# A pre-norm layer with chunked attention and a routed feed-forward on one core: the first seven feed-forward tiles computed inside the attention ticks, their pieces first in each slot

## The chip, the cores and the metric

One NeuronCore of one Trainium2 chip runs the program. Its engines are PE (TensorE), DVE (VectorE), ACT (ScalarE), POOL (GpSimd) and SP (SyncE, which here only issues DMAs). Each engine works through its own list of instructions in order, and the lists are tied together by semaphores. The metric is the device time of one execution, in microseconds, as the median of several.

## The reference

The input x is 2 x 2048 tokens of 256 values, all float32.

```python
x = x + attn(_layernorm(x))
x = x + ffn(_layernorm(x))
...
q, k, v = [silu(causal_dwconv(x @ W, conv)) for each]     # 4 taps, 256 channels, 4 heads of 64
q, k = q / norm(q), k / norm(k); beta = sigmoid(x @ Wb)
A = einsum(K * beta, K) over all heads, in chunks of 64 tokens
T = inverse of (I + tril(A, -1)); W = T @ (K * beta); U = T @ (V * beta)
scan over the chunks: u = U - W * diag(S); S = S + K^T u
    o = Q * diag(S) + tril(q . k) * u
out = (o * rsqrt(mean(o * o) + eps) * g) @ Wo
...
h = gelu(x @ Wfc) @ Wproj for 2 shared experts (all tokens)
  + the same for the 2 best of 8 routed experts (each token), weighted
```

Only the diagonal of S is used later, and `tril` of a matrix of (batch, token in chunk) keeps the token 0 of the first batch and the tokens 0 and 1 of the second. So apart from two "edge" tokens in a chunk, the output of the attention is q times the diagonal of S.

## The kernel before

The work has two stages, one behind the other.

**Attention** (0 to 613 us). The 4096 tokens go in 8 groups of 512, alternating between the two batches. Every group passes four parts, and each part is cut into 19 slots. `run_attention` (L1616) writes the same order for each engine: a *tick* runs slot 0 of all parts, then slot 1, and so on, and the parts of one tick belong to different groups. There are 11 ticks; the first three and the last three lack some parts.

- `ahead` (slots 8 to 18): statistics of the first layer norm on VectorE, the power -1/2 on GpSimd (L732), the scaled x `xn` on ScalarE (L870), its transposes `xnT` (L965), beta.
- `front` (slots 0 to 17): the projections of q, k and v in float32 (L990), their eviction twice on ScalarE, plain and scaled (L812, L813), three convolution steps on VectorE (L1278), silu (L799), the head sums of the squares (L981) and their power on GpSimd (L689), K to token layout (L972), normalized and turned back (KT), then K times beta, A (L1027), the five masked copies `CT` on GpSimd (L697), Q and V.
- `back` (slots 0 to 15): the inverse by doubling, five levels of three products: Y (L1052), Z (L1058) and its transpose ZT (L1059). Then W and U (L1065), their products with K, the sums over chunks and the scan on VectorE (slot 13, L1358 to L1386), the edge tokens, the squares of o. In slot 12 GpSimd splits one piece of the shared weights into a high and a low float16 half (L706 to L710).
- `tail` (slots 0 to 12): o to token layout, normalized, turned back, times Wo (L1106), the residual, the statistics of the second layer norm, its power (L721), `x2n`, its transposes, the router's logits (L1123).

PSUM has eight banks. The parts take theirs in turn from `Ring`s: three for front, three for back, one for tail and ahead together, and the eighth for small sums. A product waits until its bank has been emptied.

**Feed-forward** (613 to 1420 us). A tile is 256 tokens; a *unit* is a tile times one expert. An f32 product is made of three float16 products (high x high, high x low, low x high). A unit has four up groups of 12 products (L1191), each followed by gelu (L902), the high half on ScalarE (L907) and the low half on VectorE (L1555), and then 48 down products (L1206) and one eviction. There are 16 tiles for the two shared experts and 39 routed ones: 71 units. x of each tile is read back and turned on PE (L1175). `shared_order` does the first 8 shared tiles, and meanwhile splits the 32 pieces of routed weights (L929, L1564) and runs the router in nine steps on VectorE (`router`); `routed_order` does the 39 routed tiles, `shared_order` the last 8 shared ones, where the routed rows are gathered and added.

## Time and profile before

| what | us |
|---|---|
| median of 3 runs | 1411.62 (1410.79 to 1422.15) |
| the profiled execution | 1421.95 |
| its span, first to last instruction | 1420.1 |
| attention stage, up to the last logits | 613 |
| a full tick (all four parts) | 65 to 71 |
| feed-forward from its first up group | 797 |

The span is what the trace covers; the execution's time is 1.85 us more. Busy times are those of one execution. TensorE's clock has two levels here, 2.4 GHz (1.00) and 1.2 GHz (0.5); "PEclk" is its mean over a stretch. PE's "busy" counts work at either level. A matmul of float32 operands stands in the trace as two records, a transpose or a float16 matmul as one.

### The profile page before, as it was taken

How to read it: one execution, taken by the hardware profiler on the slowest of the kernel's cores; microseconds unless marked ns; L12 is line 12 of the kernel's file. 1: busy time of each engine (PE TensorE's matmuls, PEld its weight loads, DVE VectorE, ACT ScalarE, POOL GpSimd, SP SyncE). 2: the span in 40 equal slices, each digit the busy share in tenths (PEclk: the TensorE clock that was granted, in tenths of full speed). 3: DMA queues.
4: the chain of work that ended last, by engine and by line, in shares of the span. 5: the costliest groups of instructions: out<-in, count | busy, mean ns of one | idle time of the engine just before them, and what ended most of it. 6: DMA issues, size and time to landing. Idle time of an engine off the chain costs nothing.

```text
span 1420.1 us, 28215 instructions
## 1 busy us (share of the span) xinstructions
PE 1278.8 (90%) x10048; PEld 1117.9 (79%) x10049; DVE 735.0 (52%) x1258; ACT 599.2 (42%) x1081; POOL 360.5 (25%) x335
## 2 busy tenths in 40 slices
PE   4787989889898988569989999999999999999998
PEld 2667787768686867458878889899989999888887
DVE  2556656775767665327785433333333333344554
ACT  3442525252534342055636444444444444453442
POOL 0406162533334244200001022112211221043342
PEclk9787979997988889769999999999999999999999
DMA  2000101010101010043424211111111112133332
GB/s 89 30 1 30 45 30 46 30 60 15 59 15 59 0 60 29 17 129 123 158 74 150 83 38 52 50 46 44 52 51 45 44 51 52 53 106 111 111 109 76
DMA packets 60541, 86.12 MB, mean 61 GB/s; under 512 B 7168, under 2 KB 50432, under 8 KB 60480
## 3 DMA queue, kind: packets, MB, share of 16 engines
q1 hardware_dynamic: 53664, 66.65, 14.5%
q0 software_dynamic: 6816, 18.62, 4.7%
q8 instruction: 42, 0.69, 0.2%
q14 instruction: 19, 0.16, 0.0%
HBM read 60.35 MB, written 24.90 MB: 60 GB/s over the span
## 4 chain that ended last, share of the span: by engine, by line
PE 79%; DVE 8%; issue 6%; ACT 4%; POOL 3%; SPq 1%; DMA 0%; DVEq 0%; POOLq 0%; ACTq 0%
PE ps L1191 26%; PE ps L1206 25%; PE ps L990 4%; PE ps L981 3%; PE ps L965 3%; PE ps L1065 3%; PE ps L1052 2%; PE ps L1059 2%; PE ps L972 2%; PE ps L1058 2%; PE ps L1175 2%; PE ps L1106 2%; DVE W L1278 2%; POOL W L697 1%; PE ps L1143 1%
## 5 line engine op out<-in xcount | busy, mean ns | idle before, releaser
L1191 PE MATMUL ps<-late_room,W 128*128 128x256 f16 x3408 | 387.1, 274 | 7.4 <-DVE late_room L1549 7.4
L1206 PE MATMUL ps<-W,late_room 128*128 (+1 forms) x3408 | 383.2, 273 | 0.0
L1191 PEld LDWEIGHTS ps<-late_room,W 128*128 (+1 forms) x3408 | 334.8, 98 | 48.6 <-issue 4.8
L1206 PEld LDWEIGHTS ps<-W,late_room 128*128 128x128 f16 x3408 | 333.4, 98 | 38.2
L1555 DVE SCALAR_TENSOR_TENSOR late_room<-ps,late_room 128x512 f16<-128x512 f32 x284 | 189.1, 688 | 243.8 <-ACT late_room L907 243.6
L902 ACT ACTIVATE ps<-ps 128x512 f32<-128x512 f32 x284 | 165.4, 583 | 343.7 <-PE ps L1191 343.7
L907 ACT ACTIVATE late_room<-ps 128x512 f16<-128x512 f32 x284 | 161.0, 596 | 0.0
L791 ACT COPY W<-ps 128x512 f32<-128x512 f32 x144 | 82.1, 584 | 141.9 <-PE ps L965 114.2
L1278 DVE SCALAR_TENSOR_TENSOR W<-W 128x512 f32<-128x512 f32 x144 | 114.1, 793 | 24.7 <-ACT W L813 21.3
L743 POOL COPY gath<-idx 128x2 int32 (+1 forms) x39 | 7.1, 182 | 469.2 <-PE ps L1175 324.1
L965 PE MATMUL ps<-idt,W 128*128 128x128 f32 x384 | 72.7, 343 | 44.5 <-ACT W L870 17.4
L965 PEld LDWEIGHTS ps<-idt,W 128*128 128x128 f32 x384 | 59.5, 182 | 51.8 <-issue 24.3
L990 PE MATMUL ps<-W 128*128 128x512 f32 x192 | 99.7, 624 | 0.0
L746 POOL DMA_INDIRECT late_room<-x2n_d,gath x78 | 75.2, 964 | 43.5 <-POOL gath L743 31.6
L1606 DVE TENSOR_SCALAR late_room<-ps 128x512 f32<-128x512 f32 x39 | 27.0, 692 | 108.1 <-PE ps L1206 108.1
L981 PEld LDWEIGHTS ps<-W 128*128 128x128 f32 x384 | 54.2, 228 | 25.5 <-issue 14.9
L697 POOL TENSOR_TENSOR W<-W 128x512 f32<-128x512 f32 x40 | 56.7, 1451 | 66.9 <-ACT W L791 66.9
L981 PE MATMUL ps<-W 128*128 128x2 f32 x384 | 55.3, 278 | 17.8 <-ACT W L802 9.4
L772 POOL DMA_INDIRECT W<-ys_d,lastidx x64 | 61.5, 961 | 36.9 <-POOL lastidx L769 26.0
L812 ACT COPY W<-ps 128x512 f32<-128x512 f32 x48 | 27.9, 582 | 83.3 <-PE ps L990 83.2
L1052 PEld LDWEIGHTS ps<-W 128*128 128x128 f32 x320 | 44.9, 209 | 21.1 <-issue 17.1
L689 POOL TENSOR_TENSOR W<-W 128x16 f32<-128x16 f32 x16 | 46.1, 2897 | 48.6 <-ACT W L823 48.6
(141 smaller groups left out, 1413.0 us busy)
## 6 DMA issues: line engine op xcount, KB each, us to landing
wstage<-in_w_ffn SPq DMA_DIRECT2D x40, 512.0 KB, 3.7
ys_d<-late_room SPq DMA_DIRECT2D x39, 256.0 KB, 2.1
W<-in_x SPq DMA_DIRECT2D x16, 512.0 KB, 3.8
x2n_d<-W SPq DMA_DIRECT2D x8, 512.0 KB, 3.0
base_d<-W SPq DMA_DIRECT2D x8, 512.0 KB, 3.0
late_room<-x2n_d SPq DMA_DIRECT2D x16, 256.0 KB, 4.1
late_room<-base_d SPq DMA_DIRECT2D x16, 256.0 KB, 3.1
acc_d<-late_room SPq DMA_DIRECT2D x8, 256.0 KB, 5.7
```

The costliest lines, as they stand in the source:

```text
L746: pool.indirect_dma_start(out=xg[b][:, c], out_offset=None, in_=x2n_d, in_offset=bass.IndirectOffsetOnAxis(ap=gath[:, b, c:c + 1], axis=0) ...
L791: act.copy(dst, ring.bank(name)).then_inc(ring.empty(n, name)[0], 1)
L902: act.activation(ps[:, c, :], ps[:, c, :], ACT.Gelu, scale=1.0 / (X_SCALE * W_SCALE)).then_inc(gelu_done, 1)
L907: act.activation(hs[b][:, 0, 2 * c:2 * c + 2].rearrange("p f t -> p (f t)"), ps[:, c, :], ACT.Copy, scale=H_SCALE).then_inc(h_high, 1)
L965: by_tile(ring, n, name, lambda to, k: pe.transpose(to, src[:, k, d * P:(d + 1) * P], idt[:]))
L981: last = pe.matmul(dst[:, at:at + P // HD], src[:, d, k * P:(k + 1) * P], headsel, start=True, stop=True)
L990: mm = pe.matmul(to, wqkv[:, d, m * P:(m + 1) * P], xnT[:, d], start=(d == 0), stop=(d == DB - 1))
L1052: by_tile(bk, n, f"Y{s}", lambda to, k: pe.matmul(to, CT[:, s - 1, k], X[:, k], start=True, stop=True))
L1191: last = pe.matmul(ps[:, c, f * XT:(f + 1) * XT], weight(slot, d, hw, cols), xs[t.par][:, hx, d], start=(q == 0), stop=(q == len(parts) - 1))
L1206: last = pe.matmul(ps[:, 4 + b, c * D:(c + 1) * D], hs[b][:, hh, f, c * P:(c + 1) * P], weight(slot, DB + f // 4, hw, cols), start=(q == 0 ...
L1278: dve.scalar_tensor_tensor(qkvT[:, m], pre[:, m, t:t + GRP], cw[:, m, t:t + 1], qkvT[:, m], ALU.mult, ALU.add).then_inc(conv_step, 1)
L1555: dve.scalar_tensor_tensor(lo, ps[:, c, :], H_SCALE, hi, ALU.mult, ALU.subtract).then_inc(h_low, 1)
```

## The change

The attention and the order of the feed-forward are rewritten.

- **Feed-forward inside the attention.** The first half (256 tokens) of each of the groups 0 to 6 is a "fed" tile. Its x comes from `x2nT` of the tail directly, so it isn't read back and turned. One tick after its tail its eight up groups go into slots 8 to 15 (`up_piece`, two PSUM banks in turn), and one tick later its four down groups into slots 1, 3, 5 and 6 (`down_piece`). In each slot the pieces come ahead of the attention's parts, on every engine. That is 14 of the 71 units.
- **12 ticks of 16 slots**, all written out, none in a loop: tick t has ahead of group t, front of t-1, back of t-2, tail of t-3, up of t-4 and down of t-5. The scan is now in slot 2 of the tail.
- **Less attention work.** The projections take three float16 products instead of a float32 one, and give beta too, spread over its head, as a tanh (`gate`). Q, V and K times beta are no longer turned to token layout: q's norm is needed on the edge tokens alone (`edges`, its power on GpSimd behind the masks), since the rest is divided out by the last norm. The inverse keeps X and makes its transpose on PE (`XT`, evicted by ScalarE) instead of a third product. W and U become one product ZK. The last norm is spread over columns by `rms`.
- **Rings:** two banks each for front, back and tail, two for the pieces; ahead shares one of the tail's.
- **Shared weights** are split on ScalarE and VectorE in ticks 1 and 2 instead of on GpSimd.
- **Behind the attention** (`late_units`): 5 early shared tiles (10 units) with the router in eight steps, 39 routed tiles, 4 final shared tiles (8 units): 57 units and 48 turns. The last 14 pieces of routed weights are loaded and split in the first five routed units (`LOADS`), and every expert gets at least one tile. In the final tiles 8 rows a tile are combined.

The diff, cut to its core (the part classes of Tile, the SyncE lists and the layout of memory are left out):

```diff
+PROJ = 4 * DB
+PROJ_ORDER = (2, 3, 6, 7, 4, 5, 0, 1)
+CONV_ORDER = (2, 3, 4, 5, 0, 1)
...
+FED = 7
+FED_ROWS = [row_tile(n, 0) for n in range(FED)]
+REST_ROWS = [row_tile(n, 1) for n in range(FED)] + [row_tile(n, h) for n in range(FED, GROUPS) for h in range(GRP // XT)]
+EARLY = 5
+FINAL = len(REST_ROWS) - EARLY
...
+LOADS = [2] * 9 + [0] * (N_SH * EARLY - 9) + [3, 3, 3, 3, 2]
...
 FRONT_FILLS = (
-    [(f"proj{m}", "act") for m in range(3 * DB)]
+    [(f"proj{m}", "act") for m in PROJ_ORDER[:5]]
+    + [("ssq", "act")]
+    + [(f"proj{m}", "act") for m in PROJ_ORDER[5:]]
     + [(f"tokK{h}", "dve") for h in range(2)]
-    + [(f"{c}T{d}", "act") for c in ("K", "Kb") for d in range(DB)]
-    + [("AT", "act")]
-    + [(f"tokQ{h}", "dve") for h in range(2)]
-    + [(f"QT{d}", "act") for d in range(DB)]
-    + [(f"tokV{h}", "dve") for h in range(2)]
-    + [("X", "dve")]
+    + [(f"KT{d}", "act") for d in range(DB)]
+    + [("AT", "dve"), ("edges", "act"), ("X", "act")]
 )
 BACK_FILLS = (
-    [(f"{w}{s}", "act" if w == "Y" else "dve")
-     for s in range(1, LEVELS) for w in ("Y", "Z", "ZT") if (w, s) != ("Z", LEVELS - 1)]
-    + [(f"{w}T{d}", "dve") for w in ("W", "U") for d in range(DB)]
+    [("Y1", "act"), ("Z1", "dve")]
+    + [(f"{w}{s - (w == 'XT')}", "dve" if w == "Z" else "act") for s in range(2, LEVELS) for w in ("Y", "XT", "Z")]
 )
 TAIL_FILLS = (
-    [(f"otok{h}", "dve") for h in range(2)]
-    + [(f"oT{d}", "act") for d in range(DB)]
+    [(f"ZK{d}", "dve") for d in range(DB)]
+    + [("corr", "dve"), ("oss", "dve")]
+    + [(f"rms{d}", "dve") for d in range(DB)]
     + [(f"attn{h}", "dve") for h in range(2)]
     + [(f"x2nT{d}", "act") for d in range(DB)]
+    + [("logits", "dve")]
 )
-AHEAD_FILLS = [(f"xnT{d}", "act") for d in range(DB)] + [("beta", "act")]
-SLOTS_A = 19
-W_SLOT = 11
+AHEAD_FILLS = [(f"xnT{d}", "dve") for d in range(DB)]
+SLOTS_A = 16
+DOWN_SLOTS = {1: (0, 0), 3: (0, 1), 5: (1, 0), 6: (1, 1)}
+UP_SLOT = SLOTS_A - 4 * N_SH
...
+def run_attention(front, back, tail, ahead, down=None, up=None, extra=None):
+    for t in range(GROUPS + 4):
+        for slot in range(SLOTS_A):
+            for stage, n, last in ((down, t - 5, FED), (up, t - 4, FED), (back, t - 2, GROUPS), (tail, t - 3, GROUPS),
+                                   (front, t - 1, GROUPS), (ahead, t, GROUPS)):
+                if stage and 0 <= n < last:
+                    stage(slot, n, n % BATCH)
...
+            def front(slot, n, b):
+                if slot == 4:
+                    pool.wait_ge(*fr.empty(n, "ssq"))
+                    pool.tensor_tensor(ssq, ssq, minus_half[:, 0:GT * NH], ALU.pow).then_inc(rnorm, 1)
+                if slot == 9:
+                    pool.wait_ge(at_kept, n + 1)
+                    if n:
+                        pool.wait_ge(*bk.full(n - 1, f"Y{LEVELS - 1}"))
                     for s in range(1, LEVELS):
                         pool.tensor_tensor(CT[:, s - 1], AT, masks[:, s].unsqueeze(1).to_broadcast([P, GT, P]),
                                            ALU.mult).then_inc(masked, 1)
...
-                n = 2 * it + b
+                if slot == 11:
+                    pool.wait_ge(*fr.empty(n, "edges"))
+                    kept_edges = esq[:, 0:DB * GCH * (b + 1)]
+                    pool.tensor_tensor(kept_edges, kept_edges, minus_half[:, 0:DB * GCH * (b + 1)], ALU.pow).then_inc(enorm, 1)
...
-            def ahead(slot, b, it):
-                n = 2 * it + b
-                if slot == 9:
+            def ahead(slot, n, b):
+                if slot == 11:
                     pool.wait_ge(stats, 3 * n + 3)
                     pool.tensor_tensor(rstd, rstd, minus_half[:, 0:GT], ALU.pow).then_inc(rstd_ready, 1)
...
+            def back(slot, n, b):
                 if slot < 10:
                     s = slot // 2 + 1
                     if slot % 2 == 0:
-                        pe.wait_ge(masked, (LEVELS - 1) * n + s)
-                        pe.wait_ge(*(fr.empty(n, "X") if s == 1 else bk.empty(n, f"Z{s - 1}")))
-                        by_tile(bk, n, f"Y{s}", lambda to, k: pe.matmul(to, CT[:, s - 1, k], X[:, k], start=True, stop=True))
+                        if s == 1:
+                            pe.wait_ge(masked, (LEVELS - 1) * (n + 1))
+                            pe.wait_ge(*fr.empty(n, "X"))
+                        else:
+                            pe.wait_ge(*bk.empty(n, f"Z{s - 1}"))
+                        by_tile(bk, n, f"Y{s}", lambda to, k: pe.matmul(to, CT[:, s - 1, k], X[b][:, k], start=True, stop=True))
+                        if s > 1:
+                            by_tile(bk, n, f"XT{s - 1}", lambda to, k: pe.transpose(to, X[b][:, k], idt[:]))
                     else:
+                        pe.wait_ge(*bk.empty(n, f"Y{s}"))
                         if s > 1:
-                            pe.wait_ge(*bk.empty(n, f"ZT{s - 1}"))
-                        pe.wait_ge(*bk.empty(n, f"Y{s}"))
-                        if s < LEVELS - 1:
-                            by_tile(bk, n, f"Z{s}", lambda to, k: pe.matmul(to, XTr[:, k], Y[:, k], start=True, stop=True))
-                        by_tile(bk, n, f"ZT{s}", lambda to, k: pe.matmul(to, Y[:, k], XTr[:, k], start=True, stop=True))
-                if slot == W_SLOT:
+                            pe.wait_ge(*bk.empty(n, f"XT{s - 1}"))
+                        by_tile(bk, n, f"Z{s}", lambda to, k: pe.matmul(to, XTr[:, k], Y[:, k], start=True, stop=True))
...
+            def up_piece(slot, n, b):
+                if slot >= UP_SLOT:
+                    e, c = divmod(slot - UP_SLOT, 4)
+                    u = N_SH * n + e
+                    if slot == UP_SLOT:
+                        if not n:
+                            pe.wait_ge(w_split, SH_PIECES)
+                        pe.wait_ge(fed_low, n + 1)
+                    if e == 0 and c < 2 and n:
+                        pe.wait_ge(y_out, N_SH * (n - 1) + c + 1)
+                    elif 4 * u + c >= 2:
+                        pe.wait_ge(h_low, 4 * u + c - 1)
+                    up_part(u, c, e, xs[n % 2])
+            def down_piece(slot, n, b):
+                if slot in DOWN_SLOTS:
+                    e, c = DOWN_SLOTS[slot]
+                    if c == 0:
+                        pe.wait_ge(h_low, 4 * N_SH * n + 4 + 3 + e)
+                    last = down_part(e, c, e)
+                    if c == XB - 1:
+                        last.then_inc(down_done, 1)
...
+            def ahead(slot, n, b):
+                if slot == 10:
+                    dve.wait_ge(xl_in[b], 16 * (n // BATCH + 1))
                     layer_stats(n, xl, bn, mv, rstd, stats)
-                if slot == 10:
+                if slot == 11:
                     dve.wait_ge(rstd_ready, n + 1)
                     dve.scalar_tensor_tensor(nmr, mv[:, :, 0], -1.0, rstd, ALU.mult, ALU.mult).then_inc(nmr_ready, 1)
```

The removed `run_attention`:

```diff
-def run_attention(eng, front, back, tail, ahead):
...
-        for slot in range(SLOTS_A):
-            for stage, at in ((back, b), (tail, t), (front, f), (ahead, a)):
```

VectorE's new order in the slots that the prediction walks through: slot 0 tail (ZB, product with K); slots 1, 2, 4, 5, 6, 7 one convolution each of K, K, V, V, Q, Q, behind the back's addition and, in slot 2, behind the whole scan; slot 8 low half, additions of the attention output, K times beta, edges; slot 9 low half, last addition, second statistics, X's transpose; slot 10 low half, nmr2, first statistics; slot 11 low half, nmr; slot 12 low half, the edges of q; slot 13 low half, halves of xnT. ScalarE has silu in slots 2, 3, 5, 6, 7 and 8 (silu(1), for Q), tanh in slots 1 and 2, and gelu in slots 8 to 15.

## Rows read from the trace of the kernel before

**Rows 1.** The page: PE's busy time, and its clock in 40 slices
```profile
PE 1278.8 (90%) x10048; PEld 1117.9 (79%) x10049; DVE 735.0 (52%) x1258; ACT 599.2 (42%) x1081; POOL 360.5 (25%) x335
...
PEclk9787979997988889769999999999999999999999
```
**Rows 2.** Windows (stretch, length, busy PE, PEld, DVE, ACT, POOL, PEclk, DMA share, GB/s)
```profile
68.70:139.90 71.20, 58.94 (x326) 49.18 (x325) 42.03 (x73) 24.41 (x45) 23.99 (x12) 0.81 0.05 16
...
276.20:345.20 69.00, 60.64 (x360) 51.50 (x359) 45.52 (x87) 27.95 (x52) 25.73 (x14) 0.84 0.12 39
...
546.00:586.00 40.00, 27.96 (x202) 25.85 (x200) 19.29 (x44) 7.80 (x14) 11.75 (x6) 0.87 0.12 40
586.00:613.00 27.00, 14.65 (x52) 11.03 (x52) 5.07 (x15) 5.70 (x9) 3.12 (x3) 0.63 0.11 39
...
623.00:1420.00 797.00, 779.78 (x7100) 699.53 (x7100) 373.14 (x566) 368.62 (x659) 151.04 (x213) 0.99 0.25 77
```
**Rows 3.** Timeline of PE in a full tick (start, length, engine, line)
```profile
287.01 1.05 PE L1058 MATMUL ps<-W 128*128 128x128 f32 x8
287.90 1.06 PE L1059 MATMUL ps<-W 128*128 128x128 f32 x8
...
290.52 1.02 PE L990 MATMUL ps<-W 128*128 128x512 f32 x2
291.38 1.05 PE L1052 MATMUL ps<-W 128*128 128x128 f32 x8
...
298.82 0.60 PE L965 MATMUL ps<-idt,W 128*128 128x128 f32 x4
299.25 1.02 PE L990 MATMUL ps<-W 128*128 128x512 f32 x2
```
**Rows 4.** Timeline of PE at the start of the feed-forward
```profile
623.12 7.14 PE L1191 MATMUL ps<-late_room,W 128*128 128x256 f16 x48 [1.51 <-DVE late_room L1549]
630.10 0.60 PE L1175 MATMUL ps<-idt,late_room 128*128 128x128 f32 x4
630.53 5.40 PE L1191 MATMUL ps<-late_room,W 128*128 128x256 f16 x48
635.77 5.40 PE L1206 MATMUL ps<-W,late_room 128*128 128x256 f16 x48
```
**Rows 5.** Groups by line, feed-forward, ScalarE and VectorE
```profile
L1555 DVE SCALAR_TENSOR_TENSOR late_room<-ps,late_room 128x512 f16<-128x512 f32 x284 | 189.1, 688 | 243.8 <-ACT late_room L907 243.6
L902 ACT ACTIVATE ps<-ps 128x512 f32<-128x512 f32 x284 | 165.4, 583 | 343.7 <-PE ps L1191 343.7
L907 ACT ACTIVATE late_room<-ps 128x512 f16<-128x512 f32 x284 | 161.0, 596 | 0.0
```
**Rows 6.** VectorE in the attention: a group by line, then its timeline
```profile
L1278 DVE SCALAR_TENSOR_TENSOR W<-W 128x512 f32<-128x512 f32 x144 | 114.1, 793 | 24.7 <-ACT W L813 21.3
...
301.11 1.40 DVE L1250 BATCH_NORM_STATS2 W<-W 128x6 f32<-128x256 f32 x4
...
324.16 2.28 DVE L1360 TENSOR_REDUCE W<-W 128x32 f32<-128x2048 f32 x1
...
328.91 0.19 DVE L1386 TENSOR_TENSOR W<-W 128x32 f32<-128x32 f32 x1
```
**Rows 7.** ScalarE in the attention, by line
```profile
L813 ACT ACTIVATE W<-ps,W 128x512 f32<-128x512 f32 x48 | 33.3, 694 | 0.0
```
**Rows 8.** Timeline of GpSimd in a full tick
```profile
303.32 1.02 POOL L732 TENSOR_TENSOR W<-W 128x4 f32<-128x4 f32 x1 [4.25 <-DVE W L1257]
...
330.93 7.10 POOL L697 TENSOR_TENSOR W<-W 128x512 f32<-128x512 f32 x5 [9.51 <-ACT W L791]
337.99 2.92 POOL L714 TENSOR_TENSOR W<-W 128x16 f32<-128x16 f32 x1
```
**Rows 9.** Timeline of ScalarE at the first silu
```profile
31.77 1.28 ACT L799 ACT_TABLE_LOAD   x1
33.07 0.63 ACT L799 ACTIVATE W<-W 128x512 f32<-128x512 f32 x1
```

More of the change, by code:

```diff
@@ L1438, in _ @@
-            run_attention(dve, front, back, tail, ahead)
-            dve.wait_ge(logits_kept, GROUPS)
-            dve.drain().then_inc(kept, 1)
+                if slot == 13:
+                    for d in range(DB):
+                        dve.wait_ge(xnT_high, DB * n + d + 1)
+                        dve.scalar_tensor_tensor(xnT[:, 1, d], ah.bank(f"xnT{d}"), X_SCALE, xnT[:, 0, d],
+                                                 ALU.mult, ALU.subtract).then_inc(ah.empty(n, f"xnT{d}")[0], 1)
@@ L1441, in _ @@
+            run_attention(front, back, tail, ahead, down=down_piece, up=up_piece, extra=split_piece)
+            dve.wait_ge(*tl.empty(GROUPS - 1, "logits"))
+            dve.sem_inc(kept, 1)
             dve.wait_ge(route_in, 16 * ROUTE_IN)
```

1593 lines of the change are left out of this document (846 added, 747 removed).

## The prediction

> **What bounds the kernel now.** I read the busy shares first: PE is busy 90% of the span, so its work and its clock come before all else [rows 1]. The windows by stage say where that holds. From 623 us on (the feed-forward stage, 71 units) PE works 780 of 797 us at clock 0.99; nothing but fewer units makes that shorter. In the attention stage (0 to 613) a full tick (tail, back, front, ahead) takes 69.0 us, with PE busy 60.6 of them at a mean clock of 0.84 [rows 2]. "Busy" misleads there, since part of it is work at half clock. The PE timeline gives the price at full clock: 8 records of an f32 128-column product take 0.89 us (287.01 to 287.90), 2 records of a 512-column one 0.86, 4 transposes 0.43 [rows 3]. A tick counted with these prices from the code is 49 us, so about 20 of its 69 us are waits and half clock. That is the room into which the change puts feed-forward work. In this stage VectorE is busy 45.5 of 69 us, ScalarE 28, GpSimd 26 [rows 2]: none is full, and the tick is set by chains across all four.
>
> **The late stage.** One unit is 48 up and 48 down products, 5.24 us each (630.53 to 635.77), so 10.48; a turn of x is 0.43 [rows 4]. Before: 71 units 744, 55 turns 24, together 768; 29 us of the 797 are something else: the first group at half clock (7.14 instead of 5.40, and the half clock goes on until the second turn), waits for the router's VectorE work, the end. After: 57 units 597, 48 turns 21. Of the other 29 I take off 7 (PE comes warm from the last down pieces) and add 5, because the router now has 10 early units for 8 longer steps instead of 9 in 16 units. That makes 645. The routed weights no longer are all split beforehand; three pieces a unit in the first routed units fit beside a unit (by LOADS each expert's four pieces are split a unit or more before they are first needed), so I cost it at nothing. The gathers of the last stage (12 before the first combine) hold VectorE some 9 us, while PE has two groups of 5.24 it may run; 0 to 5 us, I take 0.
>
> **PE work in a tick.** Removed per group: transposes of Q, V, Kb, o (48), the 5 ZT products, half of W/U, the Q head sums, beta. Added: 16 XT and 8 rms transposes, one Z, edges. In records: 24 fewer transposes (2.6 us), 48 fewer f32 product records (5.3), some 28 fewer small ones at about 0.11 (3.1): 49 becomes 38 us [rows 3]. The projection goes from 24 records of 0.43 to 48 f16 products; by the feed-forward's 109 ns for 256 columns they are 0.22 each, 10.5 for 10.3: no change [rows 4]. The fed units add 2 x 10.48 = 21. So a full tick holds 59 us of PE at full clock. It can't be shorter than that.
>
> **The chain of a tick.** I walked through the new slots with durations of before, each engine in its order. ScalarE evictions 0.58, scaled 0.69 [rows 7], silu 0.63 [rows 9], gelu 0.58, high half 0.60, VectorE low half 0.69 [rows 5], a convolution of three steps 2.33 (3 x 0.79) [rows 6], additions from PSUM as the low half, hand-overs 0.1, behind a PE group 0.25 (a rounding: 8 records are shown as 1.05 us, the next group starts after 0.89 [rows 3]). From PE's start of slot 0:
> - Slots 0 to 3: VectorE has ZB and the K product until 5.6, waits for Z1 behind the first down piece (9.5), convolves (11.9), then has the whole scan of tail slot 2 (it was 324.2 to 329.1 [rows 6]; two more small steps, 5.8) and only then the second K convolution: 20.1. The K squares are there at 21.4. PE has done its three slots at 17.5 and waits 4 us.
> - Slots 4 to 7: PE is the limit, with 2 x 2.62 of down pieces, four products of the inverse, sums and three projections; each projection needs its bank back from ScalarE (two banks now, three before). tokK is turned at 40.2, K is turned back at 42.9. Here the down pieces are hidden by nothing but also displace nothing: without them the same slots would wait for ScalarE and the pow of 2.9.
> - Slots 8 and 9: up pieces go first on every engine. VectorE comes late (conv 1 at 47.8), does low 0, both attention adds, KbT (1024 columns; bounds 0.8 as one convolution step and 1.6 as two, I take 1.4, since it has twice the columns), the edges: 51.8. AT is on PE until 53.2, kept at 54.0. low 1, Z5, 3X-2I and the second layer statistics end at 57.2 (statistics are 1.40 plus 0.7 [rows 6]).
> - GpSimd decides the rest. Its order is rstd2, the five masks, the edge norms, rstd. From rows: 1.02, 7.10 and, for 16 columns, 2.92 [rows 8]. The edge norm of an odd group has 32 columns, which nothing in the trace shows; bounds 2.92 (as 16) and 5.84 (twice 16); 4 columns cost 1.02 and 16 cost 2.92, so by that slope 5.4, which I take. So rstd is there at 57.2 + 1.0 + 7.1 + 2.9 (5.4) + 1.1 = 69.4 (71.9).
> - VectorE stands at nmr in slot 11 for that, and low 4 is queued behind it; behind low 4, PE's up piece of slot 14. Then nmr, xn (four halves of an eviction, 2.1), its turn (2 x 0.43 and 0.25, 1.1), gelu 5 and high 5, x2nT, the halves of xnT, logits and the last up piece: PE starts the next tick at 77.3 (even) or 79.8 (odd).
>
> So a full tick grows from 69 to 78 or 80 us, with 21 us of feed-forward in it; PE is idle or at half clock for 20 again, now mostly in slots 10 to 14. The eight up pieces are hidden by the GpSimd chain; would that go, they are worth their 10.5.
>
> **Table loads.** The trace shows the load before the first silu: 31.77, 1.28 us, and silu starts at 33.07 [rows 9]. Whether gelu and silu share a table no row says. If not, slot 8 has gelu, then silu(1), slot 9 gelu again, and silu comes back in slot 2: four loads in each of the five ticks with both. I put all four in the walk; two lie in waits, two delay low 1 by about 1 us. Bounds: 0 and 5.1 us a tick; I take 1. The Trainium skill (ScalarE: Activation LUTs, What ACT_TABLE_LOAD costs and Table sets) lists gelu as the anchor of a set of its own and has a switch cost 1283 ns plus a drain of about 1380, and its rule is to batch by set, which speaks against pieces ahead of silu(1). By that price the five ticks would be up to 28 us longer in sum, near 1348 instead of 1320. This trace shows the 1.28 and, with 0.02 us between load and silu, no drain; the measurement decides.
>
> **The sum.** Until the first projection 24 (as before, beta is gone, the projection weights are split instead). Tick 1 (front alone): 48, walked in the same way; four weight splits stand in it on ScalarE and VectorE. Tick 2: 55 (it was 71.2 [rows 2], with a weight split and two pows on GpSimd and the Q and V transposes behind AT). Tick 3 (tail, no feed-forward): 67. Tick 4 (up only) 76, ticks 5 to 7: 78, 80, 78, tick 8 (no ahead, so no wait for rstd, but q_edges waits for the 5.4) 74. Tick 9 (tail, back and both kinds of pieces) 48, where it was 40.0 without them [rows 2]; tick 10 41, where the tail alone, without scan and W, was 27.0 [rows 2]; tick 11 has down pieces only, 10.5, and hides the loading of the router's constants. Hand-over 4. Together 683; with 645: a span of 1328 against 1420, or 1330 against the 1421.95 of the profiled execution, 6.5% less. The median of the runs shown is 0.7% below that execution (1411.62), so I predict 1320. What a measurement of this kernel can tell from no change is about 1%.
>
> **Rivals.**
> - A, PE becomes the bound (17%). The chain in my walk is shorter than it seems, ticks 4 to 7 shrink to 59 to 62, the others by 4 to 10. For it: PE has 59 us of work, and dense f16 work keeps clock 0.99 in the late stage [rows 2]. Against: the masks' 7.1 and the pows [rows 8] stand in one queue before rstd. Attention 577, total 1222, by the median 1214.
> - B, the waits add up more (11%): half clock in the sparse slots stretches PE's share of slots 4 to 7, six ticks get 12 us longer, 683 + 72 + 645 = 1400, by the median 1391. For it: PEclk below 9 in much of the attention stage [rows 1].
> - C, slower (6%): each piece costs its whole round trip. Up piece 1.31 + 0.25 + 0.58 + 0.60 + 0.69 = 3.4, with hand-overs 3.5; eight of them 28, down 10.5, y 1.4: 40 us a tick on top of the old one, with nothing of the attention's own chain got shorter but PE's 11. Seven ticks x 40 minus 8 x 11 = 192: 613 + 192 + 645 = 1450, median 1441. The point from which the change loses is 613 + 7y + 645 = 1420: y = 23 us a tick, hardly more than the 21 of pure PE time. Against it: PE's 20 us of waits and half clock in a tick, and two banks for up pieces.
>
> My forecast (a span of 1270 to 1370, that is 1262 to 1362) has 62%; 4% lies elsewhere. The range 1245 to 1385 leaves out most of A and C and part of B. Faster by over 1%: forecast, A, and most of B, 0.90; within 1% 0.04; slower 0.06.
>
> **What would show it.** Late stage: starts near 683, 645 long, units of 10.48. Ticks of 76 to 80 with PE busy near 65 of them; if they are 62, A; if PE idles at each up piece for VectorE's low half, C. The longest wait in a tick must be VectorE's at nmr for GpSimd's pow, after the masks; if rstd is waited for less than 2 us, my chain is wrong there. PE waits some 4 us for K's head sums. About 20 loads of tables more. GpSimd busy about 30 us a tick. Wrong would also be a first idle of over 10 us at the start of the late stage, or waits of PE for the routed weights.

## The result and the profile after

The change makes the kernel slower: 1439.51 us (median of 4 runs, 1437.88 to 1440.70) against 1413.66 for the kernel before beside it, a ratio of 1.0199 with a 95% interval of 1.0157 to 1.024. I had predicted 1320, in a range of 1245 to 1385, with 6% for slower. In this section the columns of the windows are those of [rows 2], and those of a timeline those of [rows 3].

The page of the kernel after: the engines' busy times and PE's clock in 40 slices.
```profile
PE 1182.4 (82%) x9412; PEld 1014.4 (71%) x9413; DVE 714.4 (50%) x1194; ACT 650.3 (45%) x1150; POOL 356.4 (25%) x284
...
PEclk9797968789788897889889999899999999999999
```
PE has 96 us less to do than before [rows 1], and the span is 1436.8 instead of 1420.1. So 113 us more than before go by without PE. The windows say where: one full tick (381.8 to 476.4), the attention ticks, the late stage.
```profile
381.80:476.40 94.60, 71.49 (x486) 59.10 (x485) 48.90 (x88) 44.68 (x79) 27.57 (x13) 0.82 0.09 28
53.00:759.00 706.00, 524.34 (x3591) 438.30 (x3592) 371.10 (x665) 323.08 (x572) 208.85 (x102) 0.83 0.11 34
759.00:1437.00 678.00, 637.33 (x5735) 565.87 (x5732) 322.35 (x493) 305.91 (x543) 142.81 (x170) 0.98 0.29 87
```
A full tick takes 94.6 us where it took 69.0 [rows 2]. The first instruction of ScalarE in each tick's front (L908) marks the ticks: they start at 25.5, 78.8, 131.5, 204.6, 290.5, 381.8, 476.4 and 565.7, and the late stage's first turn is at 759.4.

| us | predicted | measured | off by |
|---|---|---|---|
| start | 24 | 25.5 | +1.5 |
| ticks 1, 2, 3 | 48, 55, 67 | 53.3, 52.7, 73.1 | +9.1 |
| ticks 4 to 7 | 76, 78, 80, 78 | 85.9, 91.2, 94.7, 89.3 | +49.1 |
| ticks 8 to 11, hand-over | 177.5 | 193.7 | +16.2 |
| attention | 683 | 759.4 | +76 |
| late stage | 645 | 677.4 | +32 |

That tick in lines. PE starts its slot 0 at 379.31. The second K convolution of VectorE runs beside an addition of GpSimd, and the statistics that GpSimd waits for end at 442.3:
```profile
379.31 1.92 PE L1199 MATMUL ps<-W 128*128 128x128 f32 x8
397.67 4.29 DVE L1433 SCALAR_TENSOR_TENSOR W<-W 128x512 f32<-128x512 f32 x3
399.07 2.34 POOL L799 TENSOR_TENSOR W<-W 128x1024 f32<-128x1024 f32 x1 [11.61 <-ACT W L979]
442.10 0.17 DVE L1410 TENSOR_SCALAR W<-W 128x4 f32<-128x4 f32 x1
```
GpSimd at the end of the tick:
```profile
442.35 1.01 POOL L807 TENSOR_TENSOR W<-W 128x4 f32<-128x4 f32 x1 [21.32 <-DVE W L1410]
443.32 6.30 POOL L779 TENSOR_TENSOR W<-W 128x512 f32<-128x512 f32 x5
449.58 5.42 POOL L785 TENSOR_TENSOR W<-W 128x32 f32<-128x32 f32 x1
454.96 1.01 POOL L817 TENSOR_TENSOR W<-W 128x4 f32<-128x4 f32 x1
455.94 2.00 POOL L811 TENSOR_TENSOR W<-W 128x1024 f32<-128x1024 f32 x1
```
VectorE's nmr, ScalarE's xn and the eviction of x2nT by ScalarE:
```profile
456.00 1.95 DVE L1603 SCALAR_TENSOR_TENSOR W<-W 128x4 f32<-128x4 f32 x1 [8.22 <-POOL W L817]
457.99 2.07 ACT L1013 ACTIVATE W<-late_room,W 128x256 f32<-128x256 f32 x4 [9.52 <-DVE W L1603]
461.07 1.07 ACT L876 COPY W<-ps 128x512 f32<-128x512 f32 x2
```
and PE after it:
```profile
462.24 1.08 PE L1111 MATMUL ps<-idt,W 128*128 128x128 f32 x4 [12.91 <-issue]
464.74 1.11 PE L1111 MATMUL ps<-idt,W 128*128 128x128 f32 x4 [1.41 <-DVE W L1608]
465.65 2.77 PE L1277 MATMUL ps<-late_room,W 128*128 128x256 f16 x12
468.21 3.42 PE L1257 MATMUL ps<-W 128*128 128x8 f32 x16
471.48 2.72 PE L1277 MATMUL ps<-late_room,W 128*128 128x256 f16 x12
473.99 1.92 PE L1199 MATMUL ps<-W 128*128 128x128 f32 x8
```
The queue rstd2, masks, edge norm, rstd is the one of my walk, and the 5.42 for 32 columns is my 5.4. But PE is idle for 12.91 us before it turns xn. xn is complete at 460.1, and PE starts only at 462.24: by the code the turn waits until the bank that it shares with x2nT has been emptied, and that eviction, which ends at 462.14, stands on ScalarE behind xn and behind the gelu and the high half of an up piece. Then PE turns the two halves of xn one after the other, as there is one bank for them. The up pieces that follow, 12 products each, take 2.56 and 2.51 from start to start, where a quarter of a group of 48 is 1.31 [rows 4]: the granted clock from 462 to 474 is 0.50.

The late stage: PE's waits of over 4 us for the low half of x.
```profile
853.40 6.72 PE L1277 MATMUL ps<-late_room,W 128*128 128x256 f16 x48 [5.70 <-DVE late_room L1757]
...
896.54 7.31 PE L1277 MATMUL ps<-late_room,W 128*128 128x256 f16 x48 [4.95 <-DVE late_room L1757]
914.17 7.04 PE L1277 MATMUL ps<-late_room,W 128*128 128x256 f16 x48 [4.64 <-DVE late_room L1757]
931.55 6.89 PE L1277 MATMUL ps<-late_room,W 128*128 128x256 f16 x48 [4.66 <-DVE late_room L1757]
948.93 6.74 PE L1277 MATMUL ps<-late_room,W 128*128 128x256 f16 x48 [4.82 <-DVE late_room L1757]
```
The four from 896.54 on are the routed units with three weight pieces each, which I had costed at nothing: some 4.8 us of wait and 1.6 of half clock, four times, 25 us. ScalarE shows why, in the first of them:
```profile
893.49 1.06 ACT L1077 ACTIVATE W<-wstage 128x1024 f16<-128x1024 f32 x1 [4.07 <-DMA wstage<-in_w_ffn]
894.45 0.58 ACT L1057 ACTIVATE late_room<-ps 128x512 f16<-128x512 f32 x1
```
It waits 4.07 us for the third piece to land and splits it (L1077), and only then comes the high half of the next x (L1057), for which VectorE's low half and PE wait in turn.

### The profile page after: what moved, and what is told of

It is laid out like the page before. It is cut to its first block, busy times and chain, and to the rows that moved or that the text cites. A ratio compares the mean times of both kernels' runs of the same rounds, so it can differ in the third digit from the quotient of the medians.

```text
span 1436.8 us, 25329 instructions
## 1 busy us (share of the span) xinstructions
PE 1182.4 (82%) x9412; PEld 1014.4 (71%) x9413; DVE 714.4 (50%) x1194; ACT 650.3 (45%) x1150; POOL 356.4 (25%) x284
## 4 chain that ended last, share of the span: by engine, by line
PE 59%; issue 12%; DVE 11%; POOL 9%; ACT 5%; DMA 3%; SPq 0%; POOLq 0%; DVEq 0%; ACTq 0%
PE ps L1277 22%; PE ps L1286 20%; POOL W L779 4%; PE ps L1137 3%; PE ps L1127 2%; POOL W L785 2%; PE ps L1199 2%; DVE W L1433 2%; PE ps L1111 2%; POOL W L803 1%; PE ps L1257 1%; DMA wstage<-in_w_ffn 1%; PE ps L1206 1%; DVE W L1524 1%; PE ps L1343 1%
## 5 line engine op out<-in xcount | busy, mean ns | idle before, releaser
L1277 PE MATMUL ps<-late_room,W 128*128 128x256 f16 x3408 | 414.1, 283 | 39.3 <-DVE late_room L1757 28.9
L1022 ACT ACTIVATE ps<-ps 128x512 f32<-128x512 f32 x284 | 165.4, 583 | 395.1 <-PE ps L1277 394.8
L1111 PE MATMUL ps<-idt,W 128*128 128x128 f32 x256 | 43.7, 323 | 124.0 <-issue 55.7
L1137 PE MATMUL ps<-W 128*128 128x512 f16 x384 | 100.2, 406 | 1.5 <-DVE W L1608 1.5
L876 ACT COPY W<-ps 128x512 f32<-128x512 f32 x112 | 61.3, 588 | 60.6 <-PE ps L1199 37.3
L1199 PE MATMUL ps<-W 128*128 128x128 f32 x320 | 54.9, 327 | 35.5 <-DVE W L1482 35.5
L860 POOL DMA_INDIRECT W<-ys_d,pos_i x64 | 62.7, 979 | 69.5 <-DMA ys_d<-late_room 50.3
L1199 PEld LDWEIGHTS ps<-W 128*128 128x128 f32 x320 | 50.5, 237 | 41.3 <-DVE W L1482 39.5
L1137 PEld LDWEIGHTS ps<-W 128*128 128x128 f16 x384 | 39.9, 108 | 41.2 <-issue 11.5
L1482 DVE TENSOR_TENSOR W<-W,ps 128x512 f32<-128x512 f32 x40 | 27.3, 682 | 74.4 <-PE ps L1206 74.4
L893 ACT ACTIVATE W<-ps 128x512 f32<-128x512 f32 x48 | 28.7, 598 | 68.7 <-PE ps L1137 67.8
```

Source lines behind the costliest of these rows:

```text
L860: pool.indirect_dma_start(out=yrow[k % YROWS][:, c], out_offset=None, in_=ys_d, in_offset=bass.IndirectOffsetOnAxis(ap=pos_i[:, c, t:t + 1 ...
L1022: act.activation(up_bank(n, c), up_bank(n, c), ACT.Gelu, scale=1.0 / (X_SCALE * W_SCALE)).then_inc(gelu_done, 1)
L1111: by_tile(ring, n, name, lambda to, k: pe.transpose(to, src[:, k, d * P:(d + 1) * P], idt[:]))
L1137: last = pe.matmul(to, wp[:, hw, d, m * P:(m + 1) * P], xnT[:, hx, d], start=(q == 0), stop=(q == len(parts) - 1))
L1199: by_tile(bk, n, f"Y{s}", lambda to, k: pe.matmul(to, CT[:, s - 1, k], X[b][:, k], start=True, stop=True))
L1277: last = pe.matmul(up_bank(n, c)[:, f * XT:(f + 1) * XT], weight(slot, d, hw, cols), x_halves[:, hx, d], start=(q == 0), stop=(q == len(pa ...
```

## The experiments

"Attention" is the start of the late stage's first turn, "late" the rest of the span; both are read from the one profiled execution, while the median is over all. The runs were made in six sessions, each on one chip. In four of them PE gets its instructions slowly in the final shared tiles, in two it doesn't (the last part of this section). That is worth 35 to 40 us (less in e3), and the column "slow feed" tells it, so totals are to be compared within one kind. Runs of one session: the changed kernel; e1 to e4; e5 to e8; e9 to e12; e13 to e16; e17 and e18.

| run | median us | ratio to before (95%) | attention | late | slow feed |
|---|---|---|---|---|---|
| changed kernel | 1439.51 | 1.0199 (1.0157 to 1.024) | 759.4 | 677 | no |
| e9, the same | 1441.65 | 1.021 (1.0141 to 1.0279) | 764.6 | 676 | no |
| e17, the same | 1478.74, one run | | 764.4 | 712 | yes |
| e1 rstd early | 1427.09 | 1.0129 (1.0064 to 1.0193) | 712.3 | 712 | yes |
| e2 attention first | 1449.34, one run | | 734.4 | 713 | yes |
| e3 no pieces | 1514.10, one run | | 692.3 | 820 | yes, for 20 us |
| e4 two loads | 1451.40 | 1.0288 (1.0219 to 1.0357) | 764.3 | 685 | yes |
| e5 ahead early | 1405.92 | 0.9931 (0.9892 to 0.997) | 685.4 | 716 | yes |
| e6 all early | 1377.88 | 0.9738 (0.9672 to 0.9804) | 685.8 | 690 | yes |
| e7 paced gathers | 1427.03 | 1.0114 (1.0081 to 1.0146) | 713.6 | 710 | yes |
| e8 PE shifted | 1435.86 | 1.017 (1.0098 to 1.0241) | 714.3 | 716 | yes |
| e10 plain rows | 1383.86, one run | | 712.0 | 670 | no |
| e11 all early, attention first | 1304.43 | 0.9224 (0.916 to 0.9288) | 655.8 | 651 | no |
| e12 all early, silu | 1333.00, one run | | 679.2 | 652 | no |
| e13 as e6 | 1376.91 | 0.9727 (0.9669 to 0.9784) | 687.8 | 689 | yes |
| e14 as e1 | 1432.24, one run | | 713.9 | 716 | yes |
| e15 as e11 | 1344.53 | 0.951 (0.9464 to 0.9556) | 654.2 | 689 | yes |
| e16 as e2 | 1446.62 | 1.0253 (1.0204 to 1.0302) | 728.1 | 714 | yes |
| e18 as e10 | 1384.62, one run | | 712.8 | 670 | no (e17 beside it: yes) |

**The end of the tick.** In e1 the statistics, the pow and nmr of the group ahead get earlier slots:
```
 POOL ahead (pow of rstd)      if slot == 11  ->  6
 DVE  ahead (statistics)       if slot == 10  ->  5
 DVE  ahead (nmr)              if slot == 11  ->  8
```


> The changed kernel with the first layer norm's statistics in VectorE's slot 5 (before: 10), their power on GpSimd in slot 6 (before: 11, behind the masks and the edge norms) and nmr in slot 8. Theory Q (GpSimd's queue sets the tick): in the tick at 380.6 nmr waited until 456.0, and xn, xnT, low 4, up 6, the logits and up 7 came behind it. Without that only q_edges in slot 12 still waits for the edge norms (455.0), so the next tick starts 3 to 5 us behind 455 and not at 474: the ticks of the changed kernel get 10 to 16 us shorter, those with pieces as well as those without, in all 60 to 90 us: 1350 to 1380. Theory P (the pieces' own round trips set the tick): nmr's wait goes, the pieces stay as slow as they are, and less than 20 us are gained: 1420 to 1440.

Attention fell by 52 us (764.3 in e4, which has the same attention as the changed kernel and ran beside it, to 712.3; against the first profile's 759.4 it is 47). That is a little less than the 60 to 90 expected, and far more than the rival's 20. The total, 1427, would have pointed at the rival: 35 us of slow feed had come in. The whole step early, xn and its turn too, is e5; the edits to PE's waits protect the bank that xnT shares with the tail:
```
 ACT xn  slot 12 -> 9;  PE, ACT, DVE xnT  slot 13 -> 11
 PE, before xnT:    wait for x2nT{DB-1} of tail n-3  ->  wait for attn1 of tail n-3
 PE, before x2nT1:  + wait for ah.empty(min(n + 3, GROUPS - 1), "xnT1")
```


> As the run with rstd early, but the whole layer-norm step ahead comes early: normalising in slot 9, its two transposes on PE, the high and the low half in slot 11 (before 12 and 13), so the two transposes through the one bank stand in front of the second layer norm's and not behind it. Theory 'the end of a tick is a chain that nothing covers' (xn, two transposes through one bank, then PE at half clock): each of the five full ticks is 5 to 8 us shorter than the 82 to 87 of the run with rstd early; attention 712 becomes 670 to 685. Rival 'the chain of the second layer norm ends as late': ticks stay within 2 us, attention 705 to 712. If the final shared tiles are again fed slowly, the late stage stays at 712; without that it would be 677: total 1385 to 1400 by the first theory, 1420 to 1427 by the rival.

Attention 685.4: another 27 us, at the edge of the first theory's 670 to 685, in the same conditions of the late stage (716 against 712). Together the two moves give back 74 to 79 us of attention, about as much as the walk had missed. The full ticks take 80.3, 81.7 and 78.3 (ticks 5 to 7), which is the length that the walk had given to ticks with the queue still in them.

**Two loads a unit, and the edge queries.** e4 splits at most two routed weight pieces a unit: `LOADS = [2] * 9 + [1] + [2] * 6 + [1]`.

> The changed kernel with the last pieces of routed weights two a unit over units 10 to 16 (LOADS [2]*9+[1]+[2]*6+[1]) instead of three a unit. Theory L: in the changed kernel PE waits 4.6 to 5.0 us for x's low half in four routed units (896, 914, 932, 949) and then runs their first group at half clock (6.7 to 7.3 instead of 5.4), because the third piece waits for a buffer and its DMA and ScalarE's x high half is queued behind it. With two a unit the waits go: 22 to 27 us less, 1412 to 1418, the attention stage unchanged. Rival: the waits come from the gathers (two a tile) and stay: within 5 us of 1439.5.

Its late stage is 685 against 712 and 713 of e1 and e2 beside it, 27 us less. VectorE's low half of x makes PE wait 9.6 us in all instead of 28.9. Its 1451 is above the changed kernel's 1439 because some 35 us of slow feed came on top. e6 has it too, with everything early, and VectorE's slot 12 (edge queries) moved to 15.

> As the run before it, plus the two remedies that aim at other terms: two weight pieces a unit as in the run with two loads (that took 19 of the 29 us of waits of PE for x's low half away), and VectorE's product of the edge queries, which waits for GpSimd's edge norms, in slot 15 in place of 12, so that the low halves of the last up pieces do not stand behind it (it waited 5.8 us in an odd tick). If both terms are real, the late stage has 20 to 26 us less and the odd ticks 4 to 6 us less: 1360 to 1375, below the kernel before (1408). If the slow feeding of the final shared tiles costs what the waits for weights gave back, 1380 to 1400.

Late is 25 us shorter than in e5; attention stays at 685.8, so moving the edge queries gained nothing.

**The order, which is what the change is about.** e2 turns the stages of a slot round and nothing else:
```
-  (down, t - 5, FED), (up, t - 4, FED), (back, ...), (tail, ...), (front, ...), (ahead, ...)
+  (back, ...), (tail, ...), (front, ...), (ahead, ...), (down, t - 5, FED), (up, t - 4, FED)
```


> The changed kernel with the attention's parts ahead of the pieces in each slot, on all engines. Theory Q: the pieces' place costs little, since rstd is late anyway. In slots 8 and 9 two table loads fall away (2.6 us of ScalarE a tick), the second statistics no longer wait for low 1, and low 4 stands behind nmr either way: 2 to 4 us a tick in five ticks, 10 to 20 in all: 1420 to 1430. Theory P: with the pieces behind, the chain is freed of their round trips and a tick falls by 10 or more: 1390 or less. That the pieces stand better ahead would be above 1445.

> The changed kernel with the attention's stages ahead of the pieces in every slot, and nothing else, once more: it had attention 734 and a late stage of 713 with the stretches. Without them 734 + 678 = 1412 to 1416, a tie with the kernel before (1411); with them 1449.

Attention is 734.4 (e2) against 764.3 (e4 beside it), and 728.1 in e16. Both totals stand above the changed kernel's 1439, and e2's 1449 lies above the 1445 that was to mean that the pieces stand better ahead; the slow feed again. Where the time goes is clearer tick by tick. The first three ticks have no pieces and take up to 10 us more or less in executions of the same attention, so the last column counts from tick 5 on:

| attention, us | tick 4 | 5 | 6 | 7 | 8 to the end | 5 to the end |
|---|---|---|---|---|---|---|
| changed kernel | 85.9 | 91.2 | 94.7 | 89.3 | 193.7 | 468.9 |
| e2 | 90.2 | 82.1 | 84.7 | 82.3 | 184.1 | 433.2 |
| e16 | 86.5 | 82.0 | 84.7 | 82.3 | 184.1 | 433.1 |
| e6 | 74.1 | 80.3 | 81.6 | 78.3 | 189.0 | 429.2 |
| e11 | 74.9 | 71.4 | 71.4 | 71.5 | 181.9 | 396.1 |

The pieces ahead cost 33 to 36 us. Tick 4, which has up pieces and no down pieces, gains nothing from the other order; every tick with down pieces from 5 to 7 gains 7 to 10. So it is the place of the down pieces that costs. The other order also saves 10 of the 20 table loads, but two of them fall in tick 4, where no time was gained, so they aren't the reason. e11 and e15 ask the question again with everything early.

> As the run with everything early (1378), with the order of the stages within a slot turned round: back, tail, front, ahead, then the down and up pieces. It asks the question of the change once more, with the end of the tick out of the way. If the order is worth what it was in the first pair (attention 25 us shorter than the changed kernel), 1350 to 1360. If that gain and the one of the early step are the same gain, because both come from the chain to rstd, 1375 to 1385.

> Everything early with the attention's stages first, once more. Without the stretches 1304 again (attention 656, late 651). With them, by 'session', 1304 + 38 = 1342; by 'program' 1304. The difference in attention to everything early with feed-forward first should be the 30 us of before (656 against 686) in any session.

655.8 against 685.8 (e6, in another session), and 654.2 against 687.8 (e13) on one chip: again 30 to 34, so this gain adds to the other. e11 and e15 are one program; it beats the kernel before by 7.8% without the slow feed and by 4.9% with it. One full tick of e6 and then of e11:
```profile
336.90:418.50 81.60, 69.13 (x486) 57.91 (x486) 46.53 (x89) 44.43 (x79) 27.57 (x13) 0.88 0.08 24
```
```profile
331.00:402.40 71.40, 64.47 (x486) 54.20 (x485) 44.88 (x90) 41.38 (x78) 27.61 (x13) 0.93 0.12 38
```
The same 486 products, 4.7 us less "busy" since fewer of them run at half clock, and 5.5 us less idle. VectorE's waits for the inverse's products Z (L1485, released by PE L1206) shrink. In e6 they were, with their number and the longest,
```profile
DVE W L1485 <- PE ps L1206: 13.3, 2, 9.2
```
and in e11
```profile
DVE W L1485 <- PE ps L1206: 2.7, 2, 1.5
```
In the whole attention stage VectorE waits 74.4 us for Z in the changed kernel and 25.8 in e16. The lines show how one piece of 2.6 us grows to a wait of 9. In e6, the second K convolution, PE's next product of the inverse (Y), and PE's window after it:
```profile
353.01 4.29 DVE L1436 SCALAR_TENSOR_TENSOR W<-W 128x512 f32<-128x512 f32 x3
358.55 2.07 PE L1199 MATMUL ps<-W 128*128 128x128 f32 x8 [4.74 <-DVE W L1485]
357.00:370.00 13.00, 11.45 (x58) 9.32 (x59) 3.75 (x6) 4.84 (x9) 2.90 (x1) 0.61 0.00 0
```
and the same in e11:
```profile
343.82 2.32 DVE L1436 SCALAR_TENSOR_TENSOR W<-W 128x512 f32<-128x512 f32 x3
347.08 1.06 PE L1199 MATMUL ps<-W 128*128 128x128 f32 x8
345.00:352.00 7.00, 7.00 (x61) 6.17 (x59) 4.68 (x7) 5.42 (x12) 3.83 (x2) 1.00 0.00 1
```
With the pieces ahead, the first Z product comes 2.6 us later (VectorE waits 4.16 for it instead of 1.53). VectorE's second K convolution now falls beside GpSimd's addition and takes 4.29 instead of 2.32. PE has by then done the pieces of slots 1 and 3 and waits 4.74 us for VectorE's addition of Z, and the work behind that idle time runs at a clock of 0.61. With the attention first, a down piece fills this wait and the clock stays at 1.00. The long convolution is in every full tick of e6 and of the changed kernel, and in none of the ticks 5 to 7 of e11 and e16; what it costs by itself, apart from the piece and the half clock, wasn't tested.

**No pieces at all.** e3 takes the fed units out (FED = 0), so that the new attention runs alone.

> The new attention with no pieces in its ticks (FED 0): all 16 shared tiles behind it, 8 early and 8 final, and two pieces of weights a unit. Theory Q: GpSimd's queue stands without pieces too, ticks 3 to 7 take 70 to 76 us as tick 3 of the changed kernel (73.1), the attention ends at 620 to 650 and the rest takes 795 to 805: 1420 to 1450. So the new attention is no faster than the old one (613) though PE has 11 us less in a tick, and the pieces cost 12 to 20 us a tick for 21 us of PE work. Theory P: ticks of 58 to 66, attention end below 590, total below 1395.

Its full ticks take 76 to 81 us and its attention 692, where 620 to 650 was expected. One tick:
```profile
290.70:371.70 81.00, 55.62 (x294) 45.92 (x294) 42.24 (x76) 29.96 (x59) 25.02 (x13) 0.71 0.08 27
```
Here PE's clock is 0.71. That was the surprise of the study: the restructured attention, with nothing in its gaps, is slower than the old one (69.0 [rows 2]), though it has fewer products. 21 us of pieces (10.5 in tick 4) then add only 8 to 15 to a tick. What I had called "room" was there; what was wrong was the tick without them. The early step of e5 wasn't run without pieces.

**Table loads.** e12 is e6 with silu in the fed units in place of gelu, so its feed-forward computes another function.

> As the run with everything early, but the fed units' gelu is a silu (so their activation is another function), which should share its table with the attention's silu if the four table loads of a tick come from gelu. Then the four loads of 1.28 us are gone in five ticks; my walk put 1 us of each tick's 5.1 on the path: attention 3 to 8 us shorter than 661. If the loads are all hidden, 0; if all are on the path, 25 us.

Of the 20 loads at L885 and L1022 one is left, 24 us less for ScalarE, and attention is 6.6 us shorter (679.2 against 685.8, one execution each). So gelu and silu do not share a table, and the walk's sum of 5 us was about right. Its place was not: ticks 4 to 7 are 1 us shorter together, and the rest is gained from tick 8 on.

**Instructions that come one by one.** In e1, e2 and e4 PE was idle again and again in the last 120 us, and in e3 from 1333 to 1354, "issue" being all that the trace names. The same stretch in e17, which is the changed kernel once more:
```profile
1354.17 5.74 PE L1286 MATMUL ps<-W,late_room 128*128 128x256 f16 x47
1360.35 0.28 PE L1286 MATMUL ps<-W,late_room 128*128 128x256 f16 x1 [0.44 <-issue]
1360.47 0.38 PE L1277 MATMUL ps<-late_room,W 128*128 128x256 f16 x2
1361.77 0.60 PE L1277 MATMUL ps<-late_room,W 128*128 128x256 f16 x4 [0.92 <-issue]
1363.19 0.37 PE L1277 MATMUL ps<-late_room,W 128*128 128x256 f16 x1 [0.83 <-issue]
```
while GpSimd issues its indirect gathers without a pause:
```profile
1351.88 0.94 POOL L860 DMA_INDIRECT W<-ys_d,pos_i  x1 [49.89 <-DMA ys_d<-late_room]
1353.13 0.94 POOL L860 DMA_INDIRECT W<-ys_d,pos_i  x1 [0.30 <-issue]
```
Three ways to take it away. e7 has 4 row buffers for 8 (`ACCS, YROWS = 6, 4`), so that fewer gathers are issued ahead; e8 has `for _ in range(64): pe.wait_ge(kept, 1)` ahead of the late stage, both on top of e1.

> As the run with rstd early, but 4 row buffers in place of 8, so that GpSimd issues at most 8 gathers (10 us) ahead of VectorE's combining in place of 16 (20 us). Theory 'PE's instructions come slowly while GpSimd issues gathers without a pause': the four stretches of trickling matmuls get half as long, 45 us become 15 to 25, 1400 to 1410. Rival 'the stretches belong to the layout of this program and not to the gathers': 1427 as before. If the combining itself gets later because fewer rows are there, PE should not notice, as its banks come free from VectorE within a unit.

> As the run with rstd early, but PE executes 63 more waits on a semaphore that is already there, ahead of its late stage, which moves every later PE instruction by 63 places and costs some 3 us at most. Theory 'gathers': the stretches of trickling matmuls in the final shared tiles stay, 1424 to 1432. Rival 'place of the PE instructions in their pages': they go or move, and with them up to 45 us: 1385 to 1420.

Neither helped: late 710 and 716 against 712 in e1 (the session before). Then e10 takes plain copies of consecutive rows for the gathers, and so leaves out the gathering by position; it stands on top of e1 too:
```
-  pool.indirect_dma_start(out=yrow[k % YROWS][:, c], ..., in_offset=bass.IndirectOffsetOnAxis(ap=pos_i[:, c, t:t + 1], axis=0))
+  pool.dma_start(yrow[k % YROWS][:, c], ys_d[(2 * k + c) * P:(2 * k + c + 1) * P, :])
```


> As the run with rstd early, but in the final tiles GpSimd's 64 indirect gathers of rows are 64 plain copies of 128 consecutive rows each, of the same size from the same tensor (so the final rows are combined with wrong partners: the gathering by position is left out). Theory 'the indirect gathers starve PE of instructions': no matmul waits on 'issue', the late stage is 668 to 680, 1380 to 1392. Rival 'the DMA traffic as such': the stretches stay, 1420 to 1430. Rival 'layout of the program': either.

It was gone (late 670), but it was gone in e9, e11 and e12 on that chip too, in programs that keep the gathers, so this proved nothing.

> The changed kernel itself, unaltered, on the chip on which the experiments ran. Its first profile shows no stretch of trickling matmuls in the final shared tiles, where all eight experiments do. If that belongs to this program, it is 1435 to 1442 again, with a late stage of 677. If the stretches depend on how a kernel is placed or started and not on the program, it may come out 30 to 35 us longer, 1465 to 1475, with a late stage near 712; then the experiments' gains over it are that much larger than they seemed.

> The run with everything early once more, unaltered. The eight runs of the first two sessions all had stretches of trickling matmuls in the final shared tiles, the four of the third session had none, the changed kernel among them. Theory 'a property of the chip or the session, not of the kernel': in a session without the stretches this kernel takes 686 + 652 = 1338 to 1342, as the silu variant's late stage has it; in one with them 1376 again, and then the next runs have them too. Rival 'a property of the program': 1376 here whatever the neighbours do.

> The run with rstd early once more, in the session of the three others, to set the plain copies' 1382 against it. 'Session': 712 + 677 = 1389 without the stretches, 1424 with them. 'Program': 1424 in any case, and the plain copies were what took them away.

In the next session, on another chip, all four kernels had it, e15 among them, 40 us above e11 with the same program. The last pair, on yet another chip, tells more:

> The changed kernel a third time. It serves to tell which kind of session this is: without the stretches of trickling matmuls 1437 to 1445 and a late stage of 676, with them 1470 to 1485 and a late stage near 712.

> The plain copies in place of the indirect gathers (so the final rows are again combined with wrong partners), once more. If the run beside it shows the stretches: theory 'PE's instructions come slowly only beside indirect gathers' 1380 to 1390, late stage 670; rival 'beside any heavy DMA traffic' 1420 to 1430, late stage near 712. If the run beside it shows none, this one tells nothing new and the cause stays open.

e17 has it (late 712, 23.2 us of waits on "issue" in the final tiles) and e18 beside it has none: 1384.62, as on the chip without it. A final unit in e18, in the middle of its copies:
```profile
1302.19 5.40 PE L1284 MATMUL ps<-W,late_room 128*128 128x256 f16 x48
1307.43 5.40 PE L1275 MATMUL ps<-late_room,W 128*128 128x256 f16 x48
1312.67 5.40 PE L1284 MATMUL ps<-W,late_room 128*128 128x256 f16 x48
```
So on that chip the indirect gathers went with the slow feed, and plain copies of the same size did not. That is one pair of single executions, and e18 differs from e17 by the early rstd too, which e1 and e14 have together with the slow feed. Why some sessions show it stays open: no chip of the experiments was used in two of them.

## Why the prediction was wrong

- **"the second layer statistics end at 57.2" and rstd at "69.4 (71.9)"** were off by 5 to 6 us. In the tick shown (odd) the statistics ended at 63.0 from PE's start at 379.3, and rstd was there at 76.7. A part is one convolution: 4.29 us in place of 2.33 [rows 6], while GpSimd added 1024 columns for 2.34 beside it. I had costed VectorE alone. Another part is half clock behind PE's wait at 398.5: 16 small products (L1127) took 3.41 us there, and 1.84 ten us later. That wait, 4.74 us long, was for VectorE's addition of Z, not for the K head sums. The walk's masks (7.1) were 6.30 and the norm exact.
- **"Then nmr, xn ..., its turn ...: PE starts the next tick at 77.3 (even) or 79.8 (odd)"** is the step that failed most: 7.9 us in the walk from rstd to the next tick, 18.0 measured (456.0 to 474.0), which is 10 of the 15 us by which this tick was longer than the walk. nmr took 1.95 us beside GpSimd's 2.00 of L811; the turn of xn waited 2.2 us for the eviction of x2nT from the shared bank, where the walk had the turn first; the two halves of xn went through one bank in turn (462.24 to 467.2, 5 us, where I had 1.1); and all that PE had left ran at half clock, 8.3 us for what takes 4.2. Moving the step ahead gave 74 to 79 us back (e1, e5).
- **"PE work in a tick ... 59 us"** was right as work (e11's tick is 71.4 with 64.5 busy), but that the down pieces "displace nothing" wasn't: they delay the inverse's products, 33 to 36 us in all from tick 5 on (e2, e11, e15, e16). This is the part that belongs to the order itself. The 728 to 734 us of e16 and e2 with e9's late stage of 676 would make 1406 to 1412, level with the kernel before: worked out, not run in such conditions.
- **The ticks that lack some part** (1 to 3, and 8 to 11) came out 9 and 16 us longer in sum. With the early step (e5) ticks 1 to 3 take 157 us, 13 less than predicted, and with the attention first too (e11) the stretch from tick 8 takes 182 against 177.5. So the same two steps account for most of it. e3 shows that the new attention without pieces has full ticks of 76 to 81 us. How much of that is clock and how much chain wasn't tested by itself.
- **"three pieces a unit ... I cost it at nothing"**: 25 to 27 us (e4, e6). I had asked whether the weights come before they are used, not what stands behind their split on ScalarE and VectorE, which is the next x, while ScalarE waits 4 us for the third piece to land.
- **The late stage** otherwise: 57 units and 48 turns as counted. e11's, with two loads, is 651 against my 645.
- **Table loads**: right in the sum (5 us predicted, 6.6 measured), not in the place. Each of the 25 loads of the changed kernel took 1.28 us. Behind 22 of them the activation starts within 0.02 us, and the instruction before them had ended 0.03 us or less before, so no drain is seen.
- **Rival C** gave 1441, which is nearly the time, and is still not what happened: it had each piece cost its whole round trip, 40 us a tick, while pieces cost 8 to 15 (e3). Rival B (waits add up, six ticks 12 us longer) came nearest, with 10 to 15 in four ticks. Its mechanism, half clock in slots 4 to 7, is there, but gives the smaller part; two thirds of the excess of the tick shown stand behind rstd. The late stage's 32 us came on top, and no case had them: all my cases shared one late stage.
- **The signs** said that VectorE's longest wait in a tick must be at nmr. It was 8.2 us long, so the queue was real, but the wait for Z was 9.05. That e11 with its 1304 lies near my 1320 doesn't confirm the walk: its full ticks take 71.4 us, not 78 or 80, because the queue that the walk had in them is gone.

The Trainium skill (SBUF — State Buffer, Terms) says that VectorE and GpSimd share a port pair and that the loser blocks fully. The rows shown above agree: nmr on 4 columns took 1.95 beside an addition of 2.00, and the convolution got 1.96 longer beside one of 2.34.

## What to carry to other kernels

When independent work is woven into a chain that is bound by waits, it is safer behind the chain's instructions in every slot: here the down pieces cost 33 to 36 us ahead and filled gaps behind, while for the up pieces of tick 4 the order made no difference. Before that, look for the chain that ends the tick after the last filler; here starting the next group's layer norm two to five slots earlier was worth twice the order. A load or split that "fits beside a unit" is costed by who is queued behind it on its engines.

## What the runs showed of the hardware

- In four of six sessions PE, beside back-to-back indirect gathers by GpSimd (one each 1.25 us), got its products in runs of often 1 to 4, with idle times of up to 2.0 us between, and lost 35 to 40 us in 120. Plain copies of the same size by GpSimd, one each 0.55 us, did not do it, on a chip where the gathers did (e17, e18, one execution each). The kernel before issues 64 such gathers too, and its medians stayed at 1408 to 1414 in every session; but its PE is in a loop meanwhile and its gathers come in pairs with pauses, so which of the two spares it isn't shown.
- GpSimd's pow takes 1.01 us for 4 columns, 2.92 for 16 [rows 8], 5.42 for 32.
- A VectorE operation of 4 columns takes 1.95 us beside a GpSimd addition of 1024 columns, and 0.16 without one (L1603 in tick 0 of the changed kernel).
- A tick of 81.0 us in which PE has 294 products has a clock of 0.71 (e3); one with 486 has 0.88 in 81.6 us (e6, which has the early step as well). So part of the filler work comes free, and with it the granted clock is higher.
